# Two of VectorE's steps moved in a Mamba-2 block with a LoRA mixture: decays' product and scaling of the state's input

## What is computed

```python
proj = einsum('bsd,ed->bse', x, in_proj_w)          # gate, hBC, dt
hBC = silu(conv(hBC) + conv_b)                      # causal, 4 taps per channel
hs, Bm, Cm = split(hBC)                             # 128 heads of 64; 8 groups of B and C
dt = clip(softplus(dt + dt_bias), 0, 100)
xch = hs * dt                                       # in chunks of 128 tokens
L = exp(segsum(dt * A))                             # decays within a chunk
Y_diag = einsum('bzlhn,bzshn,bhzls,bzshp->bzlhp', Cc, Bc, L, xch)
states = einsum('bzlhn,bhzl,bzlhp->bzhpn', Bc, decay_states, xch)
Y_off = einsum('bzlhn,bzhpn,bhzl->bzlhp', Cc, prev, exp(A_cum))
g = (Y_diag + Y_off + hs * D) * silu(gate)
out = rmsnorm(g, per group of 1024) * norm_w
return einsum('bsi,oi->bso', out, out_proj_w)
```

## Time and profile before

| | |
|---|---|
| median of 3 runs | 1662.33 us (1661.66 to 1665.45) |
| the profiled execution | 1658.31 us |
| its span | 1656.8 us, granted TensorE clock 0.998 |
| busy: TensorE, VectorE, ScalarE, GpSimd | 98%, 82%, 75%, 81% |

### The profile page before, as it was taken

How to read it: one execution, slowest core, us unless ns; L and a number is a source line. 1 busy time by engine, 2 the same in 40 slices (tenths; PEclk the granted TensorE clock), 3 DMA queues, 4 the chain that set the end, 5 groups by cost and what they waited for, 6 DMA issues and landing times.

```text
span 1656.8 us, 31784 instructions
## 1 busy us (share of the span) xinstructions
PE 1618.2 (98%) x10792; PEld 1301.6 (79%) x10792; DVE 1356.9 (82%) x1667; ACT 1236.1 (75%) x2633; POOL 1346.9 (81%) x1246
## 2 busy tenths in 40 slices
PE   7999999999999999999999999999999999999998
PEld 6778878878787877878778787877778787787766
DVE  5878788887879878798888888888788887889775
ACT  5277787777877777777877778787786868778775
POOL 3148689886999779897798969988798977989798
PEclk9999999999999999999999999999999999999999
DMA  3253367554665646664665536655465465655464
GB/s 128 71 190 109 109 178 201 172 169 109 197 185 159 168 143 193 154 183 117 183 205 166 160 115 191 193 161 165 143 191 173 148 162 161 196 163 169 125 175 130
DMA packets 232527, 265.46 MB, mean 160 GB/s; under 512 B 156072, under 2 KB 157616, under 8 KB 228144
## 3 DMA queue, kind: packets, MB, share of 16 engines
q1 hardware_dynamic: 232368, 263.45, 53.7%
HBM read 162.20 MB, written 69.73 MB: 140 GB/s over the span
## 4 chain that ended last, share of the span: by engine, by line
PE 60%; POOL 16%; DVE 8%; ACT 8%; issue 7%; DMA 0%; ACTq 0%; POOLq 0%; DVEq 0%; SPq 0%
PE P L257 8%; PE P L259 7%; PE P L258 7%; PE P L466 5%; PE P L476 5%; PE P L341 4%; PE P L477 4%; PE P L334 4%; PE P L483 4%; PE P L335 4%; ACT P L579 3%; PE P L491 2%; DVE hsX L784 2%; POOL xch L1103 2%; POOL al L1206 2%
## 5 line engine op out<-in xcount | busy, mean ns | idle before, releaser
L579 ACT ACTIVATE P<-AB,SC 128x128 f32<-128x128 f32 x1016 | 305.7, 363 | 0.0
L257 PE MATMUL P<-xh,AH 128*128 128x512 f32 x656 | 268.0, 409 | 2.0 <-DVE xl L885 2.0
L784 DVE SCALAR_TENSOR_TENSOR hsX<-P,cwt,hsX 128x1023 f32<-128x1023 f32 x189 | 241.9, 1280 | 25.5 <-ACT hsX L516 21.1
L259 PE MATMUL P<-xh,AL 128*128 128x512 f32 x656 | 257.4, 392 | 0.0
L258 PE MATMUL P<-xl,AH 128*128 128x512 f32 x656 | 255.8, 390 | 0.0
L749 ACT ACTIVATE sq<-yb 128x512 bf16<-128x512 f32 x128 | 80.7, 631 | 214.0 <-DVE yb L1048 214.0
L1078 POOL TENSOR_TENSOR AL<-AR,AH 128x512 fp32r<-128x512 f32 x82 | 117.2, 1429 | 134.1 <-ACT AH L503 134.1
L476 PE MATMUL P<-OH,gTh 128*128 128x512 f32 x512 | 215.0, 420 | 2.3 <-issue 1.5
L334 PE MATMUL P<-GH,xh 128*128 128x512 f32 x512 | 200.9, 392 | 0.2 <-ACT GH L548 0.2
L854 DVE TENSOR_TENSOR EM<-P,Gt 128x1024 f32<-128x1024 f32 x127 | 154.6, 1218 | 56.5 <-ACT P L584 29.5
L335 PE MATMUL P<-GH,xl 128*128 128x512 f32 x512 | 200.5, 392 | 0.0
(11 more groups left out here) (213 smaller groups left out, 4144.8 us busy)
## 6 DMA issues: line engine op xcount, KB each, us to landing
AB<-acr_d SPq DMA_DIRECT2D x128, 512.0 KB, 5.0
half_d<-hsX SPq DMA_DIRECT2D x60, 512.0 KB, 3.5
AR<-in_wa SPq DMA_DIRECT2D x80, 256.0 KB, 2.9
TS<-in_wg SPq DMA_DIRECT2D x16, 1024.0 KB, 6.7
TS<-in_wo SPq DMA_DIRECT2D x16, 1024.0 KB, 6.4
part_d<-pl SPq DMA_DIRECT2D x64, 256.0 KB, 3.1
pl<-part_d SPq DMA_DIRECT2D x64, 256.0 KB, 2.6
al<-acc_d SPq DMA_DIRECT2D x64, 256.0 KB, 3.0
```

The costliest lines, as they stand in the source:

```text
L257: te.matmul(o, ah_, bh_, start=(first and i == 0), stop=False)
L259: r = te.matmul(o, al_, bh_, start=False, stop=(last and i == n - 1))
L579: r = se.activation(decays(m)[:, h, :], AB[m % 2][:, h, :], ACT.Relu, bias=SC[s % 2][:, c, 3, h:h + 1], scale=-1.0)
L784: ve.scalar_tensor_tensor(out=o[:, d:T], in0=raw[:, 0:T - d], scalar=cwt[:, n, 3 - d:4 - d], in1=o[:, d:T], op0=ALU.mult, op1=ALU.add).the ...
```

## The change

Only VectorE's program is edited. `dve_decay(m + 1)`, which slots without a convolution ran between the state sum and the Y sum, is run in every slot behind the gating and, where there is one, the output sum (`al`). In slots with a convolution it was there already. `dve_scaled(m + 1)` in the second slot of each group (c = 1) goes from ahead of the Off scaling to behind the state sum. Semaphores, waits and buffers stay.

```diff
--- before.py
+++ after.py
@@ -1005,7 +1005,8 @@
                     dve_blocks(m + 1)
                     if c == 1:
                         dve_output_lo(s, (0,))
-                    dve_scaled(m + 1)
+                    else:
+                        dve_scaled(m + 1)
                 if m < M:
                     if new_tiles:
                         for i in old_tiles:
@@ -1029,11 +1030,10 @@
                         ve.wait_ge(s_sa, nsa(m))
                         ve.wait_ge(s_sl, n0(m))
                         ve.tensor_tensor(S[:, :], bank("St", m), S[:, :], ALU.add).then_inc(s_st, 1)
-                    if new_tiles:
-                        for i in new_tiles if m else ():
-                            dve_conv(i)
-                    elif m + 1 < M:
-                        dve_decay(m + 1)
+                    if c == 1 and m + 1 < M:
+                        dve_scaled(m + 1)
+                    for i in new_tiles if m else ():
+                        dve_conv(i)
                     ve.wait_ge(s_y, m + 1)
                     if c:
                         ve.wait_ge(s_tp, n0(m))
@@ -1057,12 +1057,12 @@
                     ve.wait_ge(s_rst, n_)
                     ve.scalar_tensor_tensor(out=al[pc % 2][:, :], in0=bank("O", pm), scalar=rst[:, pc, 1:2],
                                             in1=al[pc % 2][:, :], op0=ALU.mult, op1=ALU.add).then_inc(s_alo, 1)
+                if m + 1 < M:
+                    dve_decay(m + 1)
                 if m < M and not new_tiles:
                     for i in old_tiles:
                         dve_silu(i)
                 if m + 1 < M:
-                    if new_tiles:
-                        dve_decay(m + 1)
                     dve_gate(m + 1)
                 if m < M:
                     ve.wait_ge(s_gth, m + 1)
```

## The result

| | before | after |
|---|---|---|
| median (6 runs each, on the same chips) | 1662.56 us (1659.72 to 1665.59) | 1669.69 us (1667.49 to 1670.54) |
| ratio, 95% interval | | 1.0040 (1.0026 to 1.0053) |
| profiled execution, its span | 1658.31, 1656.8 us | 1669.80, 1667.7 us |

The kernel became slower by 0.4%, 7 us by the medians.

What follows compares the result with a forecast made beforehand. TensorE, busy 98% of the span, was taken as the bound, so only its waits could change. Terms -3.4 + 8.4 + 4.2 - 0.7 + 0.5 gave +9.0 us: 1667.3, or about 1671 on the median's scale, range 1659 to 1677.

Steps and rivals of the forecast that it cites:

- (a): Eighth slots of even groups (slot 55): VectorE's order is the bound; TensorE's 0.48 us wait goes, 3.4 us gained.
- (c): Second slots of odd groups (57): Y sum gains nothing, late silu delays slot 58 by 1.2 us, 8.4 us lost.
- (b): Second slots of even groups (49): POOL's queue is the bound; late silu delays slot 50 by 0.6 us, 4.2 us lost.
- Eighth slot of odd groups ... cost nothing: Slots 47, then 48: transposes 0.7 us later, but hidden by POOL's queue in slot 49; 5 us if uncovered.
- rival 3: Slot 49's cover is thinner or POOL gains a stretch: 3 to 6 us more, 1674 to 1677; chance 0.14.
- Again four: Slot 49: four POOL operations still stretched by VectorE after the scaling moves; nothing taken, bounds -0.45 to +0.45 us per slot.
- Wait for `OL`: Slot 49: TensorE's 0.56 + 0.16 us wait goes, but TensorE then waits at the transposes for POOL's block; no gain.
- Second slots of the first and last group: Slots 1 and 121: bound by VectorE, 0.7 us gained together (0 to 1.5).
- where I had +0.5: Last group, no projection work left: POOL sets the pace; 0.5 us lost to shifted collisions with POOL (0 to 1).
- Rival 1: Moved scaling and one OL part escape POOL's operations, second slots' Y sums 0.9 us sooner: -3.6 us, some 1658.7; chance 0.16.
- L543's waits over 10 us: Sign of being right: ScalarE's waits for silu at its high-halves copy grow from 2.5 us to 10 or more.
- the 0.4 us that I had allowed: Sign of being wrong: POOL's add in second slots ending over 0.4 us sooner relative to TensorE means stretches were miscounted.

Runs made afterwards that it cites:

- scaled_only: The kernel before with only the state-input scaling in second slots moved behind the state sum; 1660.71 us, ratio 1.0003.
- decay_only: The changed kernel with the scaling back in its old place, so only the decays' product is moved; 1669.26 us, ratio 1.0049 to the kernel before.
- eighth_even_only: The kernel before with the decays' product behind the gating only in eighth slots of even groups; 1660.89 us, ratio 0.9976.
- before_again: The kernel before, unchanged, run once more for a second trace; 1660.09 us.

## Why the prediction was right

It gave 1671 us (1659 to 1677) and slower; the median is 1669.69. On the scale of the profiled execution the sum was +9.0 us; the trace shows +10.9, of which 2.4 us are in slot 121, whose cause is open, so +8.5 in the rest. Against the second trace of the kernel before (span 1658.6) it is +9.1. Each term against its slots:

- (a), the sort of slot 55, -3.4: measured 7 x -0.49 = -3.4. Right, by the mechanism given.
- (c), slots 57 and 58, +8.4: measured 7 x (0.11 + 1.03) = +8.0. Right, link by link; but the chain itself gave 7 x 1.03 = 7.2, as silu took 1.38 us there for its former 1.49. The 0.11 us in slot 57 is the moved scaling (scaled_only has +0.13, decay_only -0.01).
- (b), slot 50, +4.2: measured 7 x 0.54 = +3.8. Right.
- "Eighth slot of odd groups ... cost nothing": wrong in its road, nearly right in its size. I followed silu to the gating (0.7 us at the transposes) and took 0.5 us in hand. Of what is "queued behind the product" I asked only who waits for silu, not who waits for `gTl`. TensorE's St does, because of the PSUM bank, and that comes first: 0.92 us in slot 48. Slot 49 takes back 0.79, since POOL's queue holds TensorE there anyway, so the cover that I named did its work: +0.13 net, 7 times, +0.9 us. Of rival 3's mechanism, a convolution slot that hands its delay on through slot 49, this is the small part that was real.
- "Again four" stretched POOL operations, taken at nothing: right where only the scaling moves (scaled_only: four, and the slot's length the same). In after there are three, and the gain goes into 0.86 us of POOL's waiting for ScalarE's `AH`, paced by the late TensorE, which my step didn't have. Against decay_only the moved scaling costs 0.29 us in slot 49 and 0.12 in slot 57, 7 x 0.4 = 3 us by the traces; the medians of the two kernels (1669.69 and 1669.26, from two sets of runs) don't show it.
- Wait for `OL`: gone, and worth nothing, as said.
- Second slots of the first and last group, -0.7: not shown. Slots 1 and 2 have -0.5, but slot 1 alone ranges from -0.4 to +3.6 us over the kernels; in the last group slot 121's +2.4 hid everything. The other slots from 119 on add up to +0.6; in it slot 119, of sort (a), gains 0.6 and slot 120 gives 0.5 back, as in eighth_even_only too, so the slots from 122 on have +0.7, where I had +0.5. None of TensorE's waits there stands ahead of Y.

Rival 1 needed the scaling to escape POOL's operations. The Trainium skill ("SBUF — State Buffer", Who interferes with whom) says that issue order decides who blocks. The rows of slot 49 agree with that (the scaling was stretched behind a running `xch`), and they show what I had left out for the rival: an operation that is issued behind a running one doesn't slip past, it takes the next turn. The scaling began at 730.06 while `xch` ran to 730.44, took 0.93 us for its 0.68, and POOL's add of 730.40 waited for it, 1.74 us for 1.30. One stretched operation in front of the other: the collision costs both.

One piece of luck is in it. I added the 4.0 us by which the profiled execution lay under its median to the sum. The profiled execution of after lies at its own median (1669.80 and 1669.69), so between medians the change costs 7.1 us and between profiles 10.9. The sum alone gave 1667.3, 2.4 us below the measured median; with the 4.0 us it is 1.3 above. Of the difference of 3.8 us, 2.4 may be slot 121, if the other executions of after didn't have it; that, and the rest, I leave open. decay_only's 1.0049, 8.1 us of 1660.42, lies near the sum.

Of the signs of being right, these came: no wait for `OL` from VectorE, no wait for the gated block in sort (a), L543's waits over 10 us (25.4). The idle time ahead of L854 went, but that ahead of L1045 grew by 89 us and not by "about as much" as 56.5: the product's own time went out of that hole too. TensorE's wait for the gated block, "over 20", was 19.4 us; 4.5 and 1.4 us more went to L455 and L446. One sign of being wrong came as well: in slot 49 POOL's add ends 10.7 us after the slot's start, where it was 11.5, more than the 0.4 us that I had allowed. The stretches were not the reason: scaled_only keeps the 11.5, and decay_only, where the scaling is not moved, has 10.4. It is the 0.92 us by which TensorE comes late out of slot 48, the road that I had missed.

## What to carry to other kernels

An operation that fills a hole on its engine is free; moved behind the wait that made the hole, it leaves the hole empty and delays all that is queued behind it, so follow every later instruction's *end* to its reader, buffer reuse in PSUM included. Move work only in the slots where its engine, and not another's result, is what ends last, and leave ahead of it what another in-order queue is waiting for. Removing the first of two waits of one engine gains nothing while the second has another cause: find which queue feeds the last one (here GpSimd's, whose order was worth more than either of VectorE's edits that gained).

## What the runs showed of the hardware

- VectorE's operation with two inputs in SBUF and POOL's stretch each other by turns. Silu of 128 x 1024 takes 1.23 us alone and was recorded at 1.38, 1.49, 1.78 and 2.29 us; the scaling of 128 x 512 takes 0.68 alone and up to 1.77; POOL's add took 1.27 to 1.31 us in 109 of 112 slots of before and 1.74 in three, with no value between these. The product with one input in PSUM was never stretched: L854's mean is 1212 to 1218 ns in every kernel, whatever its place, and its longest took 1228 ns. When an order is shifted, such collisions move: silu's mean rose from 1460 to 1656 ns, with no instruction changed.
- The load of the output weights took 5 to 9 us from issue to use in one and the same place of the program (slot 121: 5.0 us in before_again, 6.3 in before, 9.2 in after), and is waited for. In two executions of one program it took 7.1 and 8.8 us ahead of slot 89, and the slot's length differed by 0.46 us; ahead of slot 121 the sooner load gave the longer slot, by 0.55 us.
- A PSUM bank that a late step of VectorE still reads stops the next matmul that writes there: 0.64 us at L455 and 0.20 us at L446, seven times each in after, neither of them in the seven slots of before.
- The granted clock was 0.997 to 0.999 of full speed, 2.4 GHz, over all profiled executions, so none of the differences between traces comes from it. Other runs of the kernel before on the second chip had down to 0.991, and were longer with it (1678.16 us at 0.991, 1657.95 us at 0.998).
